# State-space stage: B and C rows split on TensorE and ScalarE, a ring of five states, re-ordered front work, expert weights spilled

## The reference

```python
xn = (x - mu) / jnp.sqrt(var + 1e-05) * ln_w + ln_b
x_inner, z = jnp.split(xn @ W_in.T, 2, axis=-1)          # 512 + 512 channels
u = silu(causal depthwise conv of 4 taps(x_inner) + conv_b)
dt_low, B_ssm, C_ssm = jnp.split(u @ W_x.T, [64, 80], axis=-1)   # 64, 16 and 16 columns
dt = jnp.clip(jax.nn.softplus(dt_low @ W_dt.T + b_dt) + DT_MIN, DT_MIN, DT_MAX)
def step(h, inp):                                         # over 1024 tokens, 16 states per channel
    dA = jnp.exp(dt_t[:, :, None] * A)
    h = dA * h + (dt_t * u_t)[:, :, None] * B_t[:, None, :]
    y = jnp.einsum('bdn,bn->bd', h, C_t)
y = (y + u * D_param) * jax.nn.silu(z)
return y @ W_out.T + residual
```

## Time and profile before

| | |
|---|---|
| median of 3 runs | 3995.5 us (3995.22 to 4000.36) |
| the profiled execution | 3988.0 us, its span 3985.2 us |
| feed-forward begins | 1253.6 us |
| first scan | 2012.4 us |
| last gating of y on DVE | 3775.7 to 3778.0 us |
| experts' first DMA | 3795.7 us |
| busy over the span | PE 86%, DVE 86%, ACT 62%, POOL 64% |

### The profile page before, as it was taken

How to read it: one execution, slowest core, us unless ns; L and a number is a source line. 1 busy time by engine, 2 the same in 40 slices (tenths; PEclk the granted TensorE clock), 3 DMA queues, 4 the chain that set the end, 5 groups by cost and what they waited for, 6 DMA issues and landing times. The chain is left out here.

```text
span 3985.2 us, 64192 instructions
## 1 busy us (share of the span) xinstructions
PE 3412.2 (86%) x22940; PEld 1632.6 (41%) x22940; DVE 3439.3 (86%) x5820; ACT 2459.4 (62%) x4504; POOL 2558.9 (64%) x2390
## 2 busy tenths in 40 slices
PE   5989999999997999999778788788887888887677
PEld 2633333333333555555423333333333333333366
DVE  5778888888886999999479999898989999899866
ACT  5626666676674344444477777777777777676422
POOL 1102232332334888888488989988999999988733
PEclk8979999999998999999888988898889999898789
DMA  4894666556532111110133323233223322322232
GB/s 139 281 210 64 86 99 90 81 78 90 76 55 68 34 47 45 43 50 31 37 79 77 80 77 91 79 84 83 72 78 82 89 77 79 90 73 70 59 103 83
DMA packets 291354, 329.66 MB, mean 83 GB/s; under 512 B 37375, under 2 KB 207478, under 8 KB 291030
## 3 DMA queue, kind: packets, MB, share of 16 engines
q1 hardware_dynamic: 291038, 325.58, 35.5%
HBM read 239.58 MB, written 85.03 MB: 81 GB/s over the span
## 5 line engine op out<-in xcount | busy, mean ns | idle before, releaser
L1961 POOL TENSOR_TENSOR d_dBu<-d_dtu,d_Bn 128x1024 f32<-128x1024 f32 x384 | 903.7, 2387 | 19.8 <-DVE d_dtu L2142 19.7
L817 ACT ACTIVATE b_P<-b_pT 128x512 f32<-128x512 f32 (+1 forms) x1120 | 571.7, 576 | 298.3 <-PE b_pT L721 295.4
L1741 ACT ACTIVATE d_dA<-d_dt,d_decay 128x512 f32<-128x512 f32 x768 | 524.3, 685 | 253.6 <-DVE d_h L2069 251.8
L900 DVE CUSTOM_DVE_ANT_0 b_pS<-b_pS,mask_qk 128x512 f32<-128x512 f32 (+1 forms) x768 | 501.7, 691 | 83.1 <-PE b_pS L731 73.7
L1949 POOL TENSOR_TENSOR d_h<-d_h,d_Cn 128x2048 f32<-128x2048 f32 x112 | 511.0, 4571 | 74.4 <-ACT d_last_h L1765 45.0
L693 POOL TENSOR_SCALAR_AFFINE_SELECT b_P<-b_P 128x128 f32<-128x128 f32 (+2 forms) x608 | 192.8, 321 | 515.1 <-ACT b_P L817 503.3
L2069 DVE TENSOR_TENSOR_SCAN d_h<-d_dA,d_last_h,d_dBu 128x512 f32<-128x512 f32 x384 | 462.5, 1266 | 46.5 <-PE d_y L1606 26.8
L731 PE MATMUL b_pS<-KS,QS 99*128 99x512 bf16 (+3 forms) x1536 | 475.0, 339 | 21.0 <-PEq L85 14.1
L2069 DVE TENSOR_TENSOR_SCAN d_h<-d_dA,d_dBu 128x512 f32<-128x512 f32 x384 | 443.0, 1207 | 54.7 <-PE d_y L1606 26.4
L721 PE MATMUL b_pT<-QS,KS 118*128 118x512 bf16 (+3 forms) x1536 | 449.2, 329 | 3.1 <-ACT b_P L817 1.9
L1606 PE MATMUL d_y<-d_h,d_eye 32*32 32x512 f32 x8192 | 343.6, 700 | 31.8 <-DVE d_h L2076 31.8
(11 more groups left out here) (357 smaller groups left out, 6730.3 us busy)
## 6 DMA issues: line engine op xcount, KB each, us to landing
d_Bn<-scratch_bs SPq DMA_DIRECT2D x128, 512.0 KB, 5.0
d_Cn<-scratch_bs SPq DMA_DIRECT2D x112, 256.0 KB, 3.4
scratch_parts<-a_part SPq DMA_DIRECT2D x48, 512.0 KB, 4.1
QS<-scratch_parts SPq DMA_DIRECT2D x192, 128.0 KB, 7.4
KS<-scratch_parts SPq DMA_DIRECT2D x192, 128.0 KB, 7.9
scratch_v<-a_v SPq DMA_DIRECT2D x16, 1024.0 KB, 7.6
V<-scratch_v SPq DMA_DIRECT2D x32, 512.0 KB, 11.6
a_x<-in_L_attn_x_dram SPq DMA_DIRECT2D x16, 512.0 KB, 7.7
```

What stands on the lines that cost most here:

```text
L817: act.activation(t[:, heads[0]:heads[-1] + 1, c * CH:c * CH + w], pT[:, place % RING, 0:len(heads) * w].rearrange("p (h w) -> p h w", w=w) ...
L900: last = dve.tensor_tensor_reduce(out=pS[:, j % RING, 0:w], in0=pS[:, j % RING, 0:w], in1=K["mask_qk"][:, 0:w], scale=-1.0, scalar=-MASKED ...
L1741: act.activation(to[:, m % 2, :], dt[:, c.k % 2, m, :], ACT.Exp, scale=decay[:, m, n:n + 1]).then_inc(dA_d, 1)
L1961: pool.tensor_tensor(product(c, n)[:, 2 * j:2 * j + 2, :], dtu[:, c.k % 2, 2 * j:2 * j + 2, :], Bn[:, n // BG % 2, n % BG, :].unsqueeze(1) ...
```

## The change

1. `split_rest` and `split_lo` leave DVE. TensorE forms xb - high in the bank `pf` from two matmuls (an identity on xb, `unpick`, a negative identity, on the high part), ACT takes the middle part from there, TensorE subtracts it with a third matmul, and ACT copies the low part out (`put_lo`). The bank gets one more use per chunk, SX.
2. The state ring has five slots (HS = 5), indexed over chunks by `state(c, n)`. To make room, `mrow` is held once rather than twice, `rest` goes, and the experts' weights are written to DRAM at the start of the feed-forward stage (three DMAs ahead of the others) and read again at the start of the experts' stage, where TensorE waits for them.
3. The front work is placed anew on all engines, `keep_last` stands behind the first decay (KEEP = 0), DVE's statistics and output gating stand behind the weighing, and the second half of the output projection moves from n = 10 to n = 11 on TensorE, its gating to n = 11 on DVE.

```diff
-HS, BG, BS, CR = 4, 2, 3, 3
-LAG, KEEP, AHEAD = 2, 1, (7, 5, 4, 2)
+HS, BG, BS, CR = 5, 2, 3, 3
+LAG, KEEP, AHEAD = 2, 0, (7, 5, 4, 2)
...
+            def state(c, n):
+
+                return h[:, c.times(NS, n) % HS, :, :]
...
+                    if n == 0 and e is not None and e.k % 2 == 0:
+                        wait(sp, ag_d, e.times(2))
+                        sp.dma_start(mrow[:, GA, :], S["mod"][bass.ds(e.over(2), 1), 1, GA, :].to_broadcast([P, D])).then_inc(g_in, 16)
...
+            def split_x(q):
+                rows = slice(DR, 96)
+                wait(pe, hi_d, q.times(1, 1))
+                p = bank(q, SX)
+                pe.matmul(p[rows, :], K["ident"][rows, rows], xb[rows, :], start=True, stop=False)
+                pe.matmul(p[rows, :], unpick[rows, :], bc[rows, q.k % 2, :], start=False, stop=True).then_inc(rest_mm, 1)
+
+            def split_rest(q):
+                rows = slice(DR, 96)
+                wait(pe, mid_d, q.times(1, 1))
+                pe.matmul(front_bank(q, SX)[rows, :], unpick[rows, :], mid[rows, :], start=False, stop=True, skip_group_check=True).then_inc(front_mm, 1)
...
             run(pe, spread,
-                ({10: lambda e: output(e, 1)},
-                 {1: turn_b, 2: own_input},
+                ({11: lambda e: output(e, 1)},
+                 {1: turn_b, 3: own_input},
                  {9: lambda q: project_dt(q, 2), 13: lambda q: (project(q, GT + 1, MD + 1), project(q, GT + 2, MD + 2))},
-                 {}),
+                 {15: lambda f: turn(f, 1)}),
...
-                act.activation(mid[DR:96, :], rest[DR:96, :], ACT.Copy).then_inc(mid_d, 1)
+                act.activation(mid[DR:96, :], front_bank(q, SX)[DR:96, :], ACT.Copy).then_inc(mid_d, 1)
                 wait(act, mid_d, q.times(1, 1))
                 act.activation(bc[32:DR, q.k % 2, :], mid[DR:96, :], ACT.Copy).then_inc(mid_put, 1)
+
+            def put_lo(q):
+                p = bank(q, SX)
+                act.activation(bc[0:32, q.k % 2, :], p[DR:96, :], ACT.Copy).then_inc(act_read, 1)
...
                  {15: step_input},
-                 {6: modulate}),
+                 {6: modulate, 7: scale_bias_first}),
...
-            def split_rest(q):
...
-                dve.tensor_tensor(rest[rows, :], xb[rows, :], bc[rows, q.k % 2, :], ALU.subtract).then_inc(rest_d, 1)
...
-            def split_lo(q):
...
-                dve.tensor_tensor(bc[0:32, q.k % 2, :], rest[rows, :], mid[rows, :], ALU.subtract).then_inc(lo_d, 1)
...
             run(dve, scan,
-                ({1: gate_y, 10: lambda e: gate_out(e, 1)},
-                 {},
-                 {9: split_rest, 13: split_lo},
-                 {6: stats}),
-                weigh_before,
-                ({6: lambda e: gate_out(e, 0)},
+                ({},
                  {},
                  {},
-                 {10: clear}), first=first)
+                 {8: clear}),
+                weigh_before,
+                ({1: gate_y, 6: lambda e: gate_out(e, 0), 11: lambda e: gate_out(e, 1)},
+                 {},
+                 {},
+                 {6: stats}), first=first)
...
+            for name in ("baseT", "acatT", "bcatT"):
+                sp.dma_start(S[name], K[name][:, :, :] if name != "bcatT" else K[name][:, :]).then_inc(spilled, 16)
...
+                    for name in ("baseT", "acatT", "bcatT"):
+                        sp.dma_start(K[name][:, :, :] if name != "bcatT" else K[name][:, :], S[name]).then_inc(again, 16)
...
+            pe.wait_ge(again, 48)
```

More of the change, by code:

```diff
@@ L1538, in step @@
                     sp.dma_start(h1e[:, :, :], tiles(S["r"][tokens(c), :])).then_inc(e_in, 16)
-                if f is not None and f.k % 2 == 0:
-                    wait(sp, ag_d, f.times(2, -4))
-                    sp.dma_start(mrow[:, f.k // 2 % 2, GA, :], S["mod"][bass.ds(f.over(2), 1), 1, GA, :].to_broadcast([P, D])).then_inc(g_in[f.k // 2 % 2], 16)
             pipeline(sp, step, total, U, U, 3)
@@ L1550, in spread_c @@
                 if n == DVE_C[0]:
[L1551 removed]
+                    wait(pe, act_read, taken(c, SX))
                     wait(pe, mid_put, c.times(1, 1))
@@ L1842, in take_x @@
             def take_x(q):
-                wait(act, lo_d, q.times(1, 0))
+                if q.base * U + q.k > 0:
+                    wait(act, front_mm, taken(q.back(1), SX))
                 wait(act, b_st, q.times(16, 0))
@@ L1906, in first @@
                     grow(q)
+                    split_mid(q)
                     step_size(q)
+                    put_lo(q)
                     gate(q, 2)
@@ L1911, in first @@
                 turned(f, 0)
-                if q is not None:
-                    split_mid(q)
                 turned(f, 1)
@@ L1924, in _ @@
                  {},
-                 {1: lambda q: inner(q, 2), 7: silu, 8: take_x, 9: lambda q: below(q, 1), 10: grow, 11: split_mid, 14: lambda q: gate(q, 2)},
-                 {9: lambda f: normalise(f, 1, (0,)), 13: lambda f: (normalise(f, 1, (1,)), normalise(f, 1, (2,)), normalise(f, 1, (3,))), 15: lambda f: turned(f, 0)}),
+                 {3: lambda q: convolved(q, 0), 7: silu, 8: take_x, 11: grow},
+                 {13: lambda f: (normalise(f, 1, (2,)), normalise(f, 1, (3,))), 15: lambda f: turned(f, 0)}),
                 decays(2),
@@ L1994, in modulate @@
             def modulate(f):
-                wait(pool, m_in[f.k // 2 % 2], f.over(4, 16, 16))
+                wait(pool, m_in, f.over(2, 16, 16))
                 wait(pool, xn1, f.times(1, 1))
@@ L2029, in _ @@
                  {},
-                 {6: scale_bias_first}), first=first)
+                 {}), first=first)
         @block.vector
@@ L2068, in scan @@
                     decays, products = (dAs[:, m % 2, :], dA[:, m % 2, :]) if n in PE_B else (dA[:, m % 2, :], product(c, n)[:, m, :])
-                    dve.tensor_tensor_scan(h[:, n % HS, m, :], decays, products, start, ALU.mult, ALU.add).then_inc(scanned, 1)
+                    dve.tensor_tensor_scan(state(c, n)[:, m, :], decays, products, start, ALU.mult, ALU.add).then_inc(scanned, 1)
             def weigh(c, n):
@@ L2123, in gate_out @@
             def gate_out(e, j):
-                wait(dve, g_in[e.k // 2 % 2], e.over(4, 16, 16))
+                wait(dve, g_in, e.over(2, 16, 16))
                 wait(dve, out_mm, e.times(2, j + 1))
@@ L2128, in first_modulate @@
             def first_modulate(f):
-                wait(dve, m_in[f.k // 2 % 2], f.over(4, 16, 16))
+                wait(dve, m_in, f.over(2, 16, 16))
                 wait(dve, xn1, f.times(1, 1))
@@ L2455, in build @@
         state_space(nc, A, S, K)
+        K.update({n: k for n, k in zip(last, kept(ctx, {n + "_again": v for n, v in last.items()}).values())})
         experts(nc, A, S, K)
```

85 lines of the change are left out of this document (41 added, 44 removed).

## The result

The changed kernel is slower: 4047.6 us as the median of 4 runs (4034.1 to 4054.7), beside 3995.4 for the kernel before on the same chip (4 runs). The ratio is 1.0129, 95% interval 1.0103 to 1.0155, some 52 us. The forecast of 3928 us, its range and its sign were wrong. The profiled execution took 4049.3 us.

What follows compares the result with a forecast made beforehand. VectorE, with least idle time, was taken to bound the state-space stage: its work plus waits. Terms -35.9 - 58.8 - 6.4 + 37.6 - 7 + 0 + 3 = -67.5 us gave 3928 us, range 3888 to 3970.

Steps and rivals of the forecast that it cites:

- TensorE's products: TensorE's new split matmuls, 2.0 us per chunk, hidden in its idle time: 0, up to +32 us.
- The ring: Five state slots: all VectorE scan waits for TensorE's sums go, -58.8 us; bounds 0 to -58.8.
- Rival B: Smaller gain: half the ring's waits return as waits for GpSimd or ScalarE, 3957 us; chance 0.18.
- ScalarE: Gains put_lo and has pieces moved; VectorE's waits for its decays change by -7 us, between -30 and +30.
- VectorE's work: Two subtractions leave VectorE in the state-space stage: -35.9 us; 20.4 if only the shortest form counts.
- The projection: Second half at state 11 delays turned products, 3.45 us wait per chunk; with gating +37.6 us net.
- rival C: Slower: TensorE's low clock lasts into the projection at state 11, adding 83 us, 4011 us; chance 0.08.
- rival A: Larger gain: state 11's wait is shared, ScalarE and GpSimd catch up, 38 us less, 3890 us; chance 0.25.
- The statistics: VectorE's statistics stand some 2.9 us later, behind n = 6's weighing and gating; their wait goes: -6.4 us.
- The ends: Spill DMAs at feed-forward start, pipeline filling and reloads at the experts' start: together +3 us.

Runs made afterwards that it cites:

- e6: Kernel before with only the spilled expert weights and single set of modulation rows; ring of four, order and VectorE's subtractions as before: 3999.5 us, ratio 1.0039.
- e5: Kernel before with ring of five, spilled expert weights and single set of modulation rows; order and VectorE's subtractions as before: 3994.0 us, ratio 1.0014.
- e12: e5 without VectorE's two subtractions, the middle part a copy of the whole rows, the low part zero: 3973.6 us, ratio 0.9949.
- e13: e12 with the low part put by ScalarE behind the gate of state 12, as a copy without the difference: 3987.2 us, ratio 0.9994.
- e2: Changed kernel with the order of before on all engines; split by TensorE and ScalarE, ring of five and spill kept: 4024.9 us, ratio 1.0094.
- e10: Changed kernel without TensorE's three difference products; ScalarE keeps its three narrow pieces in place but copies from xb: 4032.6 us, ratio 1.0101.
- e11: Changed kernel with two wide filler products ahead of each of the four step-size products of states 8 and 9: 4105.9 us, ratio 1.0282.
- e7: Changed kernel with the split given back to VectorE as its two subtractions, new order and ring of five kept: 3997.2 us, ratio 1.0035.
- e9: e8 with spills issued behind the feed-forward's first loads, and TensorE's wait for reread weights just before their first product: 3992.1 us, ratio 1.0001.
- e14: e9 without VectorE's two subtractions, the middle part a copy, the low part zero: 3976.1 us, ratio 0.9968.
- e8: e7 with the output projection's second half back at state 10 and its gating behind state 10's scans: 3994.5 us, ratio 1.0019.

## Why the prediction was wrong

From before to after there is a ladder: e6, e5, e12, e13, e2, after. Its steps are single but for two. The step to e2 brings TensorE's products, a further use of the shared bank, and earlier places for two of ScalarE's pieces (`split_mid` one decay earlier, `put_lo` two). The last step is the whole new order. In us of 3987, each uncertain by 7 to 13:

```
step                                     measured   predicted
spill and single row set   (e6)            +15.5        +3 (with the fill)
ring of five               (e6 to e5)      -10.0       -58.8
no subtractions on VectorE (e5 to e12)     -25.9       -35.9
low part on ScalarE        (e12 to e13)    +17.9        -7 (with its new order)
TensorE's products         (e13 to e2)     +39.9         0
new order                  (e2 to after)   +14.0       +31.2 (+37.6 - 6.4)
sum                                        +51.4       -67.5
```

**The ring (-58.8, the largest error)** failed in its mechanism. The waits for the sums were real and did go, but decays arrive hardly sooner: at state 4 VectorE waited 2.0 us for the sums in e6 and 1.7 for ScalarE in e5. Rows 3 give a wait to the one that came last and are silent on the one just behind. Rival B named this and returned half; in fact five sixths came back. The lower bound of the term, 0, was nearer than the value taken. In e5 the sums were still waited for 15.5 us of the 1600; only the new order took all of that wait away.

**TensorE's products (0)** is the other error that decides the sign. The hiding was counted by TensorE's 358 us of idle time and by its own readers in the next chunk. But TensorE works its queue in order too, and in the same chunk the products stand ahead of what VectorE needs. In e2 it stands so at state 11 (TensorE; then the same place in e13, which has no such products):

```profile
2994.51 1.14 PE L1615 MATMUL d_y<-d_h,d_eye 32*32 32x512 f32 x32
2995.53 1.01 PE L1703 MATMUL d_f<-d_xb,ident 32*32 32x512 f32 x2
2996.38 0.37 PE L1704 MATMUL d_f<-d_bc,d_unpick 32*32 32x512 bf16 x1
2996.69 1.09 PE L1608 MATMUL d_dA<-ident,d_dBu 128*128 128x128 f32 x8
```
```profile
2966.00 1.14 PE L1615 MATMUL d_y<-d_h,d_eye 32*32 32x512 f32 x32
2967.07 1.09 PE L1608 MATMUL d_dA<-ident,d_dBu 128*128 128x128 f32 x8
```

The turned products come 1.1 us later, and so does the first scan of state 11: VectorE stands 2.04 us before it (named "issue", but its decay had ended 3.6 us before and the turned products had just come; in every second chunk the like wait is named after them), where in e13 it stands 0.93. The round trip on ScalarE looks worse than it is:

```profile
2996.79 0.59 ACT L1879 ACTIVATE d_mid<-d_f 32x512 bf16<-32x512 f32 x1 [2.94 <-PE d_f L1704]
2998.07 0.72 ACT L1764 ACTIVATE d_dAs<-d_dt,d_decay 128x512 f32<-128x512 f32 x1
3006.95 0.60 ACT L1863 ACTIVATE d_z<-d_f 128x512 f32<-128x512 f32 x1 [2.37 <-PE d_f L1680]
```
```profile
2997.44 1.22 DVE L2098 TENSOR_TENSOR_SCAN d_h<-d_dAs,d_dA 128x512 f32<-128x512 f32 x1 [2.04 <-issue]
2998.89 3.65 DVE L2098 TENSOR_TENSOR_SCAN d_h<-d_dAs,d_dA 128x512 f32<-128x512 f32 x3 [0.23 <-ACT d_dAs L1764]
3008.16 1.22 DVE L2098 TENSOR_TENSOR_SCAN d_h<-d_dA,d_dBu 128x512 f32<-128x512 f32 x1 [2.26 <-ACT d_dA L1764]
```

`split_mid` waits 2.94 us for the difference, but the decay behind it is late for VectorE by only 0.23 us. The other wait, 2.26 us at state 12, is for a decay behind a piece of the gate, for which ScalarE waited 2.37 us, and this goes with the clock. In this chunk the granted clock is 0.72 over states 11 and 12. In the one chunk of e2 where it stayed at 1.00 the four scans of state 12 run without a wait, though all the products are there; in e13 it is 1.00 there in every chunk behind the first, and the wait at state 12 at most 0.6 us (e2 with the low clock, e2 with the full one and its scans of state 12, e13):

```profile
2998.00:3010.00 12.00, 9.76 (x50) 3.58 (x50) 9.41 (x9) 8.46 (x17) 9.14 (x3) 0.72 0.13 34
```
```profile
2322.00:2334.00 12.00, 8.42 (x55) 3.29 (x54) 11.66 (x10) 10.72 (x21) 9.87 (x4) 1.00 0.08 27
2326.55 4.78 DVE L2098 TENSOR_TENSOR_SCAN d_h<-d_dA,d_dBu 128x512 f32<-128x512 f32 x4
```
```profile
2968.00:2980.00 12.00, 7.80 (x54) 3.17 (x53) 11.49 (x10) 10.06 (x19) 11.07 (x5) 1.00 0.10 30
```

From e13 to e2 states 11 and 12 wait 2.4 us more a chunk, 39 us over 16, which is the step's 39.9: half of it is the products' place ahead of the turned products; the other half goes with the low clock, as far as single chunks can show it. Why the clock falls there is open. Where the places of ScalarE's pieces are the same, in the new order (e10 to after), the products cost 11 us. The size was off too: in the changed kernel they take 3.05 us a chunk, not 2.0, since they run at the low clock (in e2 and e11, mostly at the full one, 1.9 and 1.8 us):

```profile
L1703 PE MATMUL d_f<-d_xb,ident 32*32 32x512 f32 x30 | 28.2, 1042 | 13.0 <-ACT d_dt L1893 13.0
L1704 PE MATMUL d_f<-d_bc,d_unpick 32*32 32x512 bf16 x15 | 9.4, 629 | 0.0
L1709 PE MATMUL d_f<-d_mid,d_unpick 32*32 32x512 bf16 x15 | 8.2, 544 | 0.0
```

**ScalarE (-7)** had the wrong sign. Its busy time, 1287.7 of 1816 us, makes it look idle, but what it puts ahead of a decay is on the path. The prediction put most of its 30.1 us of waits before at state 9; counted by state it was 14 us, and 4.7 lay before the first scan. The bound of +30, every split piece uncovered, covers the +17.9 of e13. The 26 us from e7 to e10 are net of the subtractions that go; with the 13 us that these were worth in the new order (e9 to e14) ScalarE's pieces cost some 39 us there, above the bound.

**VectorE's work (-35.9)** was right in mechanism and kind: VectorE's own time fell by 41.8 us. What is lost again goes mostly to GpSimd at state 0 (1.4 of the 1.9 us a chunk by which the waits rise from e5 to e12), whose floor was seen but taken as 75 us away.

**The projection (+37.6)** was right in mechanism: state 11 waits 4.7 us instead of 1.7, 48 us over 16 chunks. With the clock at 1.00 the wait was 3.28 us (e7), the predicted 3.45 within 0.2; the rest is the low clock that lasts into the projection's first half, part of rival C. But the wait is shared, as rival A said: taking it away in e8 gave 6 us. The new order as a whole costs 8 to 14 us.

**The statistics (-6.4)** were right: that wait is gone. GpSimd's wait for them fell only from 41.3 to 22.2 us, not "mostly".

**The ends (+3)** were mis-sized: 12 us in the profile. TensorE starts the feed-forward 4.7 us late, and 5.4 us of waiting for x stand there that moving the spills behind the first loads removes.

The forecast added terms with the full length of the waits that go, and zeros for all that other engines could still do to VectorE. The first made -95 of it unsafe, the second hid +58. Rival C gave the right sign and some of the cause. Its own sign, output products with a median near 600 ns, did not come (the median is 379), and its 83 us were too much for the projection; but the low clock costs about 1 us a chunk at state 10 and 1.4 at state 11 (4.7 less 3.3), some 38 us of the 91.9 by which VectorE's waits rose. That is an estimate from waits, and since waits cover each other the time to be won would be less; no run has the changed kernel at the full clock without another cost. The sum of rival C also counts the low clock for one of two turned products on its path; with both it is 5.8 us a chunk, not 5.2.

## What to carry to other kernels

A wait row names the last to arrive; before counting it as gain, look how far behind the second one is, for that is all that can be won. With four engines that are each waited for in a chunk, freeing the busiest pays only a part (11 to 26 of 36 us here). New instructions on an engine with idle time are not free either: they delay what stands behind them in that engine's queue (here 1.1 us a chunk of turned products), and on TensorE they can go with a lower clock for all that follows (here another 1.2 us a chunk). Ask of each new instruction who stands behind it, not how much idle time its engine has, and look in every chunk at the granted clock beside the wait: single chunks that kept the full clock priced it here without a further run.

## What the runs showed of the hardware

A 32-row piece of 512 columns takes ScalarE 0.57 to 0.63 us, while 128-row ones take 0.57 to 0.72: the rows left out save next to nothing. A 32-row float32 product of 512 columns took TensorE 1.04 us a pass in the stretch of the changed kernel, where the granted clock around it was 0.50, and 0.58 us in e2 and e11 at 1.00; a bf16 one took 0.63 and 0.37 us. Wide filler products kept the granted clock at 1.00 at state 9 where the same queue without them had 0.50. Chunks of one kernel with the same queue differ in the clock: of the 15 chunks of e2 beside which a front is made, one had 1.00 over states 11 and 12 and no wait at state 12; the others had 0.5 to 0.9 and waits of 1.2 to 2.8 us.
